# Second layer's dense pass with two buffers of turned rows, and shared score banks for the narrow diagonal heads of the first attention

## Chip, cores and metric

One core of a Trainium2 chip runs the whole program in one launch. The metric is the device time in microseconds (us). All products are float32: most are split into a high and a low part of a rounded 32-bit type (fp32r) and computed as three matmuls, high by high, low by high and high by low.

## What is computed

Two layers over 2048 rows of 512 numbers, each an attention and a feed-forward part with a layer norm after each. The change touches the first attention and the dense pass ahead of the second.

```python
# layer 0: 16 heads of 32, causal
scores = jnp.einsum('bhqd,bhkd->bhqk', q, k).astype(jnp.float32) * scale
causal = jnp.tril(jnp.ones((S, S), dtype=bool))
scores = jnp.where(causal, scores, jnp.finfo(jnp.float32).min)
attn = jax.nn.softmax(scores, axis=-1)
out = jnp.einsum('bhqk,bhkd->bhqd', attn, v)
...
# layer 1: one head of width 512, not causal, rotary in blocks of 128
q = (x @ q_w.T + q_b) * scale
kv = x @ kv_w.T + kv_b
k, v = (kv[..., :E], kv[..., E:])
q = _rope(q)
k = _rope(k)
```

## The kernel before

A tile is 128 rows, a chunk is 512 rows or four tiles; 2048 rows are 16 tiles or four chunks. Every engine has its own instruction stream, written out by hand, and semaphores order the streams. An engine takes its instructions strictly in the order written, so one that waits holds back all behind it.

**The first attention (layer0_attention).** There are 16 items, a query chunk c with a group g of four heads. A planner (attention0_plan) lists the steps of each item: step i scores one key tile kt against the item's 512 queries for the four heads, and the order interleaves four kinds of work. "scores" computes the transposed scores of one head (L838) into one of three banks, stb; "unit" computes a 128-row block of scores (L817) into another three banks, from which VectorE takes row maxima (L740, L745); "av" multiplies exponentials with values (L855), and "den" sums them (L876). Of the 160 steps 64 lie on the diagonal, 16 of each kind d = kt - 4c = 0, 1, 2, 3: they score 512, 384, 256 or 128 queries. On a diagonal step each head gets a second matmul (L843), which adds the mask of one 128x128 triangle by means of the identity matrix. ScalarE takes the exponential of each head from its bank (L702), and a head's first matmul waits until the exponential three heads back is done, which frees the bank. The av of step i-1 stands ahead of the fourth head of step i. GpSimd adds the exponentials of two steps (L668). The mask and the identity are fp32r.

**The dense pass (first part of layer1_attention).** First the layer norm of each tile: VectorE statistics (L906, L908), ScalarE root (L912), VectorE factors (L1846, L1848), ScalarE apply (L1696, in place in X). Then "turn": TensorE transposes the four 128x128 blocks of a tile (L1993) into a bank tb, ScalarE rounds them into the high part xch (L1705), VectorE subtracts for the low part xcl (L1854). xch and xcl hold one chunk. From a chunk TensorE computes eight "pieces" (12 matmuls each, 128 outputs by 512 rows, banks qk) and four "values" (12 matmuls each, 128 rows by 512, banks vb). Two pieces make a pair p. For each pair ScalarE copies both halves out with the bias (out, L1716), GpSimd multiplies by the cosines (L1657), VectorE by the sines (L1867), VectorE combines (L1874, L1875), ScalarE rounds (high, L1730), VectorE subtracts (low, L1884). Queries go to DRAM (L1616), keys stay in kth and ktl, and values go through the two buffers of vhl (L1738, L1888) to DRAM (L1605). The cosines and sines of a chunk, cs, have one buffer: SyncE loads those of the next chunk (L1624) behind the query stores of the chunk's fourth pair.

TensorE's order per chunk: eight pieces, turns n and n+1 of the next chunk, this chunk's values n-2 and n-1, turns n+2 and n+3, the next chunk's values n and n+1. A turn into xch waits for all pieces of the chunk before and for the value of the tile that it overwrites:

```python
if c > 0:
    act.wait_ge(s["qk_ok"], c * 2 * NP)
    act.wait_ge(s["v_ok"], k - TC + 1)
```

A piece waits until the copy and the sines of the piece four back are done, since it reuses that bank; a transposition waits for its tile's norm and for the low part of the tile two back; a value waits for the low part of the value two back.

Of the kernel before, what the change touches and what calls it, by code (L numbers as in the profile page):

```python
# [15 lines left out]
F32 = mybir.dt.float32  # L16
# [144 lines left out]
def layer0_qkv(nc, xT, w_qk, w_v, rope, masks, eye, X, V, hi, lo, qst, consts, qk_dram):  # L161
    with ExitStack() as ctx:
# [3 lines left out]
        maskf = m.sb("maskf", [P, P])  # L166
# [15 lines left out]
                 "t1_ok sin_ok sum_ok hi_ok lo_ok hstore0 hstore1 lstore0 lstore1 consts early0 early1").split()  # L182
# [34 lines left out]
        def _(sp):  # L217
# [16 lines left out]
            sp.dma_start(maskf[:], masks[:, 1, :]).then_inc(s["consts"], 16)  # L234
# [54 lines left out]
        def _(act):  # L289
# [17 lines left out]
            for what, c, j in acts:  # L307
# [33 lines left out]
                elif what == "v":  # L341
                    act.wait_ge(s["v_ok"], k + 1)
                    nc.scalar.activation(V[:, k, :], vb[:, k % 2, :], ACT.Copy).then_inc(s["vs_ok"], 1)
                    if k == TC:
                        act.wait_ge(s["consts"], 48)
                        nc.scalar.activation(identr[:], ident[:], ACT.Copy)
                        nc.scalar.activation(maskr[:], maskf[:], ACT.Copy)

        @block.vector
        def _(dve):  # L350
# [11 lines left out]
            nc.vector.memset(hidden[:, 0:CH - P], 0.0)  # L362
            split_half(0)
# [75 lines left out]


# [105 lines left out]
def layer0_attention(nc, stage_before, stored, landed, qx, qk_dram, m_dram, xs_dram, acc_dram, token, V, X, hi, lo, qst, consts, early, out_w, first_o):  # L546
# [14 lines left out]
    q_loads = [len([o for o in range(EARLY, n + 1) if q_slot[o] == q_slot[n]]) for n in range(NI)]  # L561

    with ExitStack() as ctx:
# [31 lines left out]
        def _(sp):  # L595
            def k_in(n, j, after):
                if after >= 0:
                    sp.wait_ge(s["st_ok"], 4 * (after + 1))
# [4 lines left out]
            def q_in(n, after):  # L603
                if after >= 0:
                    sp.wait_ge(s["st_ok"], 4 * (after + 1))
# [39 lines left out]
        def _(pool):  # L645
# [12 lines left out]
            for ev in order:  # L658
                if ev[0] == "av" and ev[1] % 2 == 0 and ev[1] + 1 < len(steps) - 1:
# [3 lines left out]
                    for a in range(2):  # L663
                        hs = slice(2 * a, 2 * a + 2)
                        pool.wait_ge(s["exp_ok"], 4 * (i + 1) + 2 * a + 2)
# [22 lines left out]
        def _(act):  # L688
            for ev in order:
                if ev[0] == "scores":  # L690
# [3 lines left out]
                    k = 4 * i + h  # L694
                    act.wait_ge(s["st_ok"], k + 1)
                    if i >= PSLOTS and h == 0:
# [5 lines left out]
                    nc.scalar.activation(probs[:, i % PSLOTS, h, w0:], stb[:, k % 3, w0:], ACT.Exp, scale=SCALE0)\  # L702
                        .then_inc(s["exp_ok"], 1)
# [7 lines left out]
                elif ev[0] == "prep":  # L711
                    k = ev[1]
                    if k == 0:
                        act.wait_ge(s["wo_in"], 16)
                        act.wait_ge(s["st_ok"], 4 * (final[NI - 2] + 1))
# [72 lines left out]
        def _(pe):  # L788
# [12 lines left out]
            for ev in order:  # L801
# [23 lines left out]
                elif ev[0] == "scores":  # L825
# [4 lines left out]
                    k = 4 * i + h  # L830
# [5 lines left out]
                    if k >= 3:  # L836
                        pe.wait_ge(s["exp_ok"], k - 2)
                    last = nc.tensor.matmul(  # L838
                        stb[:, k % 3, w0:],
                        kst[slot_of[n, kt // TC] % KSLOTS][0:97, h, kt % TC * P:(kt % TC + 1) * P],  # L840
                        qs[q_slot[n]][0:97, h, w0:], start=True, stop=kt < TC * c)
                    if kt >= TC * c:
                        last = nc.tensor.matmul(stb[:, k % 3, w0:w0 + P], identr[:], maskr[:], start=False, stop=True)  # L843
                    last.then_inc(s["st_ok"], 1)
                elif ev[0] == "av":
# [5 lines left out]
                    pe.wait_ge(s["exp_ok"], 4 * i + 4)  # L851
# [1728 lines left out]
```

## Time and profile before

| | |
|---|---|
| median of 3 runs | 2250.15 us (2246.75 to 2253.99) |
| the profiled execution: time | 2249.26 us |
| the profiled execution: span of the trace | 2247.5 us |
| TensorE busy | 2159.9 us, 96% |
| VectorE, ScalarE, GpSimd busy | 1180.8, 747.3, 669.3 us |
| first attention, 166 to 738 us | 572 us |
| dense pass after its first values, 1155.5 to 1311.6 us | 156.1 us |
| mean granted TensorE clock | 0.984 |

Matmuls overlap, and the end of each is modelled; so the text reads the distance from one start to the next start rather than a matmul's duration. A matmul that follows a wait is listed from about the moment the wait ended, with the load of its weights still ahead of it.

### The profile page before, as it was taken

The page shows a single profiled execution, that of the slowest core. Times are in us where ns is not written, and L with a number is a line of the kernel's source. Part 1 is how long each engine was busy: PE and PEld are TensorE (multiplying, and loading weights), DVE is VectorE, ACT ScalarE, POOL GpSimd, SP SyncE. Part 2 cuts the span into 40 slices and gives each one's busy share as a digit, 9 for nine tenths or more (in the row PEclk, how much of TensorE's full clock was granted, in tenths as well). Part 3 has the DMA queues.
Part 4 walks back from the last instruction along what each step waited for, and adds up shares of the span by engine and source line. Part 5 has one row for each costly group of instructions (what it writes and reads, how often), then busy time and mean ns, then how long its engine had stood idle before and what let it go on. Part 6 is the DMA issues. An engine that isn't in the chain of part 4 may idle for free. (4 is left out here: it accounts for less than half of the span.)

```text
span 2247.5 us, 27475 instructions
## 1 busy us (share of the span) xinstructions
PE 2159.9 (96%) x10148; PEld 1495.4 (67%) x10148; DVE 1180.8 (53%) x2305; ACT 747.3 (33%) x1344; POOL 669.3 (30%) x458
## 2 busy tenths in 40 slices
PE   7999999999999999999989999999999999999997
PEld 6866555555553654444477778888887888888886
DVE  5877777766662653222255642223235546554666
ACT  3425555555557322111144421111123211211223
POOL 4354555655557114432232340000003021212100
PEclk9989999999999999999999999999999999999999
DMA  5578345433310625655444350001101010100001
GB/s 181 185 195 198 96 124 126 103 85 72 67 29 21 251 107 220 138 95 92 75 133 150 131 215 23 25 19 29 38 1 57 1 38 20 38 19 26 12 19 57
DMA packets 104604, 197.27 MB, mean 88 GB/s; under 512 B 10384, under 2 KB 27664, under 8 KB 103056
## 3 DMA queue, kind: packets, MB, share of 16 engines
q1 hardware_dynamic: 92064, 162.78, 24.6%
q0 software_dynamic: 11408, 29.69, 5.8%
q10 hardware_dynamic: 1008, 3.15, 0.4%
q8 instruction: 78, 1.28, 0.2%
q14 instruction: 46, 0.38, 0.1%
HBM read 123.82 MB, written 71.75 MB: 87 GB/s over the span
## 5 line engine op out<-in xcount | busy, mean ns | idle before, releaser
L702 ACT ACTIVATE a_probs<-a_stb 128x512 f32<-128x512 f32 (+3 forms) x640 | 309.7, 535 | 238.5 <-PE a_stb L843 125.4
L668 POOL TENSOR_TENSOR a_probs<-a_probs 128x1024 f32<-128x1024 f32 (+3 forms) x158 | 277.9, 1772 | 245.7 <-PE a_avb L855 231.7
L740 DVE TENSOR_REDUCE a_mparts<-a_sbank 128x1 f32<-128x512 f32 x384 | 240.0, 683 | 86.3 <-PE a_sbank L817 85.9
L2220 POOL CAST m_wh<-wst 128x1024 fp32r<-128x1024 f32 x24 | 26.6, 1110 | 719.7 <-POOLq L1537 368.6
L57 PE MATMUL m_gu<-hi,m_wh 128*128 128x512 f32 x512 | 200.4, 391 | 3.0 <-DVE m_h L2350 1.6
L59 PE MATMUL m_gu<-hi,m_wl 128*128 128x512 f32 x512 | 199.8, 390 | 0.0
L58 PE MATMUL m_gu<-lo,m_wh 128*128 128x512 f32 x512 | 199.7, 390 | 0.0
L855 PE MATMUL a_avb<-a_probs,V 128*32 128x512 f32 (+3 forms) x1280 | 150.4, 542 | 0.7 <-ACT a_probs L702 0.7
L2299 DVE TENSOR_TENSOR m_h<-m_sg,m_gu 128x512 f32<-128x512 f32 x63 | 43.3, 687 | 193.8 <-ACT m_sg L2250 193.5
L745 DVE CUSTOM_DVE_ANT_0 a_junk<-a_sbank,hidden 128x128 bf16<-128x128 f32 (+3 forms) x256 | 113.2, 488 | 56.5 <-PE a_sbank L817 55.1
L2250 ACT ACTIVATE m_sg<-m_gu 128x512 f32<-128x512 f32 x64 | 38.3, 599 | 262.6 <-PE m_gu L59 262.6
L817 PE MATMUL a_sbank<-hi,q 96*128 96x512 f32 (+3 forms) x304 | 118.7, 415 | 5.8 <-DVE a_mparts L740 4.2
L838 PE MATMUL a_stb<-q,hi 97*128 97x512 f32 (+3 forms) x304 | 121.5, 408 | 1.4 <-ACT a_probs L702 1.1
L1822 ACT ACTIVATE pth<-q_tb 128x512 fp32r<-128x512 f32 x64 | 38.2, 598 | 246.2 <-PE q_tb L2079 246.2
L1959 DVE TENSOR_TENSOR ptl<-q_tb,pth 128x512 fp32r<-128x512 f32 x64 | 44.1, 691 | 143.4 <-ACT pth L1822 143.4
L817 PE MATMUL a_sbank<-lo,q 96*128 96x512 f32 (+3 forms) x288 | 109.1, 403 | 5.4 <-DVE a_mparts L740 3.3
L838 PE MATMUL a_stb<-q,lo 97*128 97x512 f32 (+3 forms) x288 | 110.3, 398 | 2.4 <-ACT a_probs L702 2.1
L57 PEld LDWEIGHTS m_gu<-hi,m_wh 128*128 128x128 f32 x512 | 96.5, 188 | 23.8 <-DVE m_h L2350 2.0
L58 PEld LDWEIGHTS m_gu<-lo,m_wh 128*128 128x128 f32 x512 | 96.6, 189 | 20.0
L59 PEld LDWEIGHTS m_gu<-hi,m_wl 128*128 128x128 f32 x512 | 96.4, 188 | 20.2
L1308 POOL DMA_INDIRECT acc<-e_rows_b,X x37 | 57.8, 1563 | 164.3 <-DVE e_rows_b L1432 131.2
L57 PE MATMUL q_vb<-vh,pth 128*128 128x512 f32 x256 | 102.6, 401 | 2.7 <-DMA vl<-v 2.7
(292 smaller groups left out, 4734.8 us busy)
## 6 DMA issues: line engine op xcount, KB each, us to landing
qk<-v_hl SPq DMA_DIRECT2D x32, 512.0 KB, 3.1
hi<-qk SPq DMA_DIRECT2D x60, 256.0 KB, 5.1
lo<-qk SPq DMA_DIRECT2D x60, 256.0 KB, 5.4
wst<-in_w_mlp SPq DMA_DIRECT2D x24, 512.0 KB, 3.5
q<-qk SPq DMA_DIRECT2D x42, 256.0 KB, 5.9
xs<-a_zeros POOLq DMA_DIRECT2D x39, 264.0 KB, 2.8
X<-xs SPq DMA_DIRECT2D x39, 264.0 KB, 2.7
v<-vhl SPq DMA_DIRECT2D x16, 512.0 KB, 5.3
```

Of the source, the lines that this page charges most:

```text
L57: nc.tensor.matmul(out, wh, xh, start=start, stop=False, skip_group_check=True)
L58: nc.tensor.matmul(out, wh, xl, start=False, stop=False, skip_group_check=True)
L59: return nc.tensor.matmul(out, wl, xh, start=False, stop=stop, skip_group_check=True)
L668: nc.gpsimd.tensor_tensor(probs[:, i % PSLOTS, hs, w0:], probs[:, i % PSLOTS, hs, w0:], probs[:, (i + 1) % PSLOTS, hs, w0:], ALU.add)\
L702: nc.scalar.activation(probs[:, i % PSLOTS, h, w0:], stb[:, k % 3, w0:], ACT.Exp, scale=SCALE0)\
L740: nc.vector.reduce_max(to, sbank[:, b, :], AX).then_inc(s["unit_max"], 1)
L745: nc.vector.tensor_tensor_reduce(out=junk[:, k % 2, 0:w], in0=sbank[:, b, 0:w], in1=hidden[:, CH - w:CH], scale=1.0, scalar=BIG, op0=ALU.a ...
L817: nc.tensor.matmul(bank[:, 0:w], qs[q_slot[n]][0:96, h, t * P:(t + 1) * P], kst[at % KSLOTS][0:96, h, 0:w], start=True, stop=True)\
L838: last = nc.tensor.matmul(stb[:, k % 3, w0:], kst[slot_of[n, kt // TC] % KSLOTS][0:97, h, kt % TC * P:(kt % TC + 1) * P], qs[q_slot[n]][0: ...
L855: last = nc.tensor.matmul(avb[HD0 * h:HD0 * (h + 1), w0:], V[:, kt, g * P + h * HD0:g * P + (h + 1) * HD0], probs[:, i % PSLOTS, h, w0:], ...
L1308: nc.gpsimd.indirect_dma_start(acc_dram[:, :], bass.IndirectOffsetOnAxis(ap=to[:, j:j + 1], axis=0), y[:, j % 2, :], None, compute_op=ALU. ...
L1959: nc.vector.tensor_tensor(ptl[:, 4 * g:4 * g + 4, :].rearrange("p a b -> p (a b)"), tb[:, (g + 1) % 2, :], f32(pth[:, 4 * g:4 * g + 4, :]) ...
```

## The change

In the dense pass a second pair of buffers holds turned rows: the part of kth and ktl that belongs to the last chunk's keys, which is written last. Even chunks use it, odd chunks use xch and xcl. A turn no longer waits for the pieces of the chunk before; from chunk 2 on it waits for the values of two chunks back. The order on TensorE per chunk becomes: pair 0, value, pair 1, turns n and n+1, value, pair 2, turns n+2 and n+3, pair 3, the other two values. Chunk 0 has only values 2 and 3 beside it, and chunk 3 only 12 and 13, with 14 and 15 after the first scores as before. ScalarE's, VectorE's and SyncE's orders follow.

In the first attention, steps with d=2 put two heads in one bank and steps with d=3 all four. The mask comes first, one matmul of 512 columns that reads the triangle and 128 columns of zeros repeatedly (d=2) or the triangle four times (d=3), and the heads' scores are added to it. One exponential of 512 columns then serves the bank. Semaphore counts go by banks ("groups") instead of heads. Identity and mask are bf16 now, the mask is 256 columns wide, and VectorE clears its second half once.

```diff
+        spare = [a[:, :, (NC - 1) * CH:] for a in (kth, ktl)]
+        def xc(c):
+            return spare if c % 2 == 0 else (xch, xcl)
+        def beside(c):
+            if c == 0:
+                return [2, 3]
+            return range(c * TC, c * TC + (TC if c + 1 < NC else 2))
...
+                if 1 <= p % NP < 3:
+                    v_out(beside(c)[p % NP - 1])
...
-                    for k in range(c * TC + 2, min(c * TC + TC + 2, NT)):
+                    for k in (*beside(c)[2:], *((NT - 2, NT - 1) if c + 1 == NC else ())):
                         v_out(k)
...
-                if c > 0:
-                    act.wait_ge(s["qk_ok"], c * 2 * NP)
-                    act.wait_ge(s["v_ok"], k - TC + 1)
+                if c >= 2:
+                    act.wait_ge(s["v_ok"], (c - 1) * TC)
... ScalarE, per chunk, as far as there is a next chunk
+                root(n); out(i); out(i + 1); apply(n); root(n + 1); high(p); apply(n + 1); value(v[0])
+                out(i + 2); out(i + 3); root(n + 2); apply(n + 2); turn(n); turn(n + 1); root(n + 3)
+                high(p + 1); apply(n + 3); value(v[1]); out(i + 4); out(i + 5); turn(n + 2); turn(n + 3)
+                high(p + 2); out(i + 6); out(i + 7); high(p + 3); value(v[2]); value(v[3])
... VectorE, per chunk
+                stats(n); sines(p); apply(n); stats(n + 1); sums(p); apply(n + 1); low(p); value(v[0])
+                sines(p + 1); stats(n + 2); sums(p + 1); apply(n + 2); stats(n + 3); turn(n); turn(n + 1)
+                apply(n + 3); low(p + 1); value(v[1]); sines(p + 2); sums(p + 2); turn(n + 2); turn(n + 3)
+                low(p + 2); sines(p + 3); sums(p + 3); low(p + 3); value(v[2]); value(v[3])
... TensorE, per chunk
+                for pair_no in range(NP):
+                    piece(2 * NP * c + 2 * pair_no)
+                    piece(2 * NP * c + 2 * pair_no + 1)
+                    if pair_no == 0:
+                        value(v[0])
+                    elif pair_no == 1:
+                        if more:
+                            turn(n)
+                            turn(n + 1)
+                        value(v[1])
+                    elif pair_no == 2 and more:
+                        turn(n + 2)
+                        turn(n + 3)
+                if more:
+                    for k in v[2:]:
+                        value(k)
... first attention
+def score_groups(items, steps):
+    group, done = {}, [0]
+    for i, (n, kt) in enumerate(steps):
+        per = {2: 2, 3: GH}.get(kt - TC * items[n][0], 1)
+        for h in range(GH):
+            group[i, h] = (done[-1] + h // per, h % per, per)
+        done.append(done[-1] + GH // per)
+    return group, done
...
-                    if k >= 3:
+                    if k >= 3 and j == 0:
                         pe.wait_ge(s["exp_ok"], k - 2)
...
+                    if per > 1 and j == 0:
+                        nc.tensor.matmul(stb[:, k % 3, :].rearrange("p (h n) -> p h n", h=per), identr[:],
+                                         maskr[:, 0:wide].unsqueeze(1).broadcast_to([P, per, wide]), start=True, stop=False,
+                                         skip_group_check=True)
+                    if per > 1:
+                        last = nc.tensor.matmul(stb[:, k % 3, j * wide:(j + 1) * wide], keys, asked, start=False, stop=j == per - 1,
+                                                skip_group_check=True)
...
-                                         (("hidden", CH, F32), ("identr", P, F32R), ("maskr", P, F32R)))
+                                         (("hidden", CH, F32), ("identr", P, BF16), ("maskr", 2 * P, BF16)))
```

The engines' orders are shown joined with semicolons here; in the code each call has its own line, and those on tiles n to n+3 are left out in chunk 3.

## Rows read from the trace of the kernel before

**Rows 1.** Windows: stretch, us, busy and instructions per engine, PEclk, DMA share, GB/s.

```profile
166.00:738.00 572.00, 551.87 (x3447) 292.44 (x3447) 371.99 (x901) 323.03 (x677) 319.51 (x216) 0.99 0.38 91
1155.50:1311.60 156.10, 147.81 (x649) 120.03 (x648) 97.80 (x155) 63.89 (x99) 57.60 (x40) 0.97 0.38 131
1187.80:1193.40 5.60, 5.60 (x13) 4.38 (x14) 3.02 (x4) 1.77 (x4) 0.00 (x0) 0.50 0.77 234
```

**Rows 2.** Timeline of TensorE from chunk 0 to 1: start, us, instruction, idle before.

```profile
1177.30 1.03 PE L1993 MATMUL q_tb<-ident,X 128*128 128x128 f32 x8
1178.09 0.47 PE L57 MATMUL q_vb<-q_wh,q_xch 128*128 128x512 f32 x1
...
1183.43 0.39 PE L59 MATMUL q_vb<-q_wh,q_xcl 128*128 128x512 f32 x1
1185.36 1.23 PE L1993 MATMUL q_tb<-ident,X 128*128 128x128 f32 x8 [1.54 <-DVE q_xcl L1854]
1187.76 0.76 PE L57 MATMUL q_vb<-q_wh,q_xch 128*128 128x512 f32 x1 [1.17 <-DVE vhl L1888]
...
1193.45 0.47 PE L58 MATMUL q_vb<-q_wl,q_xch 128*128 128x512 f32 x1
```

**Rows 3.** Timeline of TensorE from chunk 1 to 2.

```profile
1225.90 1.23 PE L1993 MATMUL q_tb<-ident,X 128*128 128x128 f32 x8 [1.56 <-DVE q_xcl L1854]
1228.30 0.76 PE L57 MATMUL q_vb<-q_wh,q_xch 128*128 128x512 f32 x1 [1.18 <-DVE vhl L1888]
...
1230.99 0.47 PE L57 MATMUL q_vb<-q_wh,q_xch 128*128 128x512 f32 x1
```

**Rows 4.** Groups by line, dense pass: busy us, mean ns, idle before.

```profile
L1657 POOL TENSOR_TENSOR q_turned<-q_qkf,q_cs 128x512 f32<-128x512 f32 x32 | 46.9, 1470 | 114.2 <-ACT q_qkf L1716 114.2
L1696 ACT ACTIVATE X<-X,minus,norm_rstd 128x512 f32<-128x512 f32 x12 | 9.5, 812 | 5.6 <-DVE minus L1848 5.6
```

**Rows 5.** Timeline of all engines, from chunk 0 to 1.

```profile
1188.14 1.63 SPq L1616 DMA_DIRECT2D q<-qhl  x2
...
1189.86 0.46 SPq L1624 DMA_DIRECT2D q_cs<-in_rope  x1
...
1199.81 0.75 DVE L1867 SCALAR_TENSOR_TENSOR q_across<-q_qk,bqk,q_cs 128x512 f32<-128x512 f32 x1 [0.97 <-ACT q_qkf L1716]
...
1206.36 1.04 ACT L1730 ACTIVATE qhl<-q_turned 128x1024 fp32r<-128x1024 f32 x1
```

**Rows 6.** DMA issues ahead of chunks 1 and 3: KB each, median us to landing.

```profile
q_cs<-in_rope SPq DMA_DIRECT2D x1, 512.0 KB, 5.0
...
q_cs<-in_rope SPq DMA_DIRECT2D x1, 512.0 KB, 7.2
```

**Rows 7.** Timeline of TensorE, wide heads, with and without a mask.

```profile
390.70 0.39 PE L838 MATMUL a_stb<-q,lo 97*128 97x512 f32 x1
...
390.99 0.45 PE L817 MATMUL a_sbank<-hi,q 96*128 96x512 f32 x1
391.28 0.39 PE L838 MATMUL a_stb<-q,lo 97*128 97x512 f32 x1
...
416.74 0.40 PE L838 MATMUL a_stb<-q,hi 97*128 97x512 f32 x1
...
417.21 0.40 PE L838 MATMUL a_stb<-q,hi 97*128 97x512 f32 x1
```

**Rows 8.** Timeline of TensorE, narrow heads of a step with d=3.

```profile
412.99 0.27 PE L838 MATMUL a_stb<-q,lo 97*128 97x128 f32 x1
413.10 0.28 PE L843 MATMUL a_stb<-maskr,identr 128*128 128x128 f32 x1
413.43 0.33 PE L838 MATMUL a_stb<-q,lo 97*128 97x128 f32 x1
```

**Rows 9.** Groups by line and shape, exponentials of the first attention.

```profile
L702 ACT ACTIVATE a_probs<-a_stb 128x512 f32<-128x512 f32 x448 | 243.1, 600 | 138.6 <-PE a_stb L838 107.7 <-PE a_stb L843 28.1
...
L702 ACT ACTIVATE a_probs<-a_stb 128x128 f32<-128x128 f32 x64 | 16.7, 278 | 33.7 <-PE a_stb L843 32.8
```

More of the change, by code:

```diff
@@ L693, in _ @@
                     w0 = max(0, kt - TC * items[n][0]) * P
[L694 removed]
+                    k, j, per = group[i, h]
+                    if j < per - 1:
+                        continue
                     act.wait_ge(s["st_ok"], k + 1)
[L696 removed]
+                    if i >= PSLOTS and h == per - 1:
                         act.wait_ge(s["av_ok"], i - PSLOTS + 1)
@@ L1928, in _ @@
             for c in range(NC):
-                n, p = (c + 1) * TC, c * NP
-                for t, tiles in enumerate(((n,), (n + 1, n + 2), (n + 3,))):
-                    sines(p + t)
-                    for k in tiles if c + 1 < NC else ():
-                        stats(k)
-                    sums(p + t)
-                    for k in tiles if c + 1 < NC else ():
-                        apply(k)
-                    low(p + t)
-                sines(p + 3)
-                if c + 1 < NC:
+                n, p, more = (c + 1) * TC, c * NP, c + 1 < NC
+                v = beside(c)
+                if more:
+                    stats(n)
+                sines(p)
+                if more:
+                    apply(n)
+                    stats(n + 1)
+                sums(p)
+                if more:
+                    apply(n + 1)
+                low(p)
+                value(v[0])
+                sines(p + 1)
+                if more:
+                    stats(n + 2)
+                sums(p + 1)
+                if more:
+                    apply(n + 2)
+                    stats(n + 3)
                     turn(n)
                     turn(n + 1)
-                sums(p + 3)
-                if c + 1 < NC:
-                    value(n - 2)
-                    low(p + 3)
-                    value(n - 1)
+                    apply(n + 3)
+                low(p + 1)
+                value(v[1])
+                sines(p + 2)
+                sums(p + 2)
+                if more:
                     turn(n + 2)
                     turn(n + 3)
-                    value(n)
-                    value(n + 1)
+                low(p + 2)
+                sines(p + 3)
+                sums(p + 3)
+                low(p + 3)
+                if more:
+                    for k in v[2:]:
+                        value(k)
                 else:
-                    low(p + 3)
                     peak(0)
```

135 lines of the change are left out of this document (67 added, 68 removed).

## The prediction

> **What bounds the kernel now.** I read the page first: TensorE is busy for 96% of the span, the others for 53% at most. A busy TensorE is not one at its peak, so next I read windows of the two stretches that the change touches, and in them the distances between starts. In the dense pass TensorE is busy for 147.8 of 156.1 us, while VectorE has 97.8 us of work and ScalarE 63.9 [rows 1]. So TensorE sets the end, and what others cost is only what it waits for them. The timeline shows where: at each of the three passages from a chunk to the next, ahead of turns n+2 and n+3 and ahead of the value behind them. In the first attention TensorE has 551.9 us in 572, VectorE 372, GpSimd 320, ScalarE 323 [rows 1]; there too I count its matmuls first and its waits second.
>
> **Dense pass: what is removed.** The value matmul at 1183.43 is the 24th since 1178.09, so their distance is 5.34/23 = 0.23 us, and the next instruction could start at 1183.66. The turns start at 1185.36: 1.70 us late. Eight transpositions take 0.79 us when nothing is waited for (1177.30 to 1178.09), here the value behind them starts 2.40 us after them: 1.61 us more [rows 2]. Together 3.3 us. Behind it the granted clock is 0.50, which is 1.2 GHz of 2.4 [rows 1]: from 1187.76 to 1193.45 lie 13 matmuls in 5.69 us, at full clock 13 x 0.23 = 3.0, so 2.7 us more [rows 2]. From chunk 1 to 2 the two waits are the same (1.56 and 1.18 us listed as idle, against 1.54 and 1.17), and six matmuls take 2.69 us instead of 1.4: 1.3 us more [rows 2, 3]. The third passage shows the same waits and no fall of the clock. The sum is 3 x 3.3 + 2.7 + 1.3 = 13.9 us. No matmul is added or removed here: 32 pieces, 14 values and 48 transpositions stay.
>
> The waits arise because the turns of the next chunk begin only when the last piece is through, and ScalarE and VectorE then have the last pair, two turns and a value to handle in one queue. With the second buffer the turns stand within the chunk, 2.7 to 8 us of matmuls apart from what reads them, and a value's low part is due two values later. If the other engines keep up, all 13.9 us go.
>
> **Dense pass: what is late next.** I follow the chain from the last piece of chunk 0, called time 0. Two things that before lay in the passage's slack now matter. First, cs has one buffer and SyncE asks for the next chunk's only behind the query stores of the fourth pair. That pair still has to pass ScalarE's copy, GpSimd (1.47 us a half), two VectorE sums (about 1.3 together), high (1.04) and low (1.2): about 5.3 us, more with a pair of other work in the queues. Behind it come two store issues (1.63 together) and the cs issue [rows 4, 5]. I put the issue at 7 us (before it was at 1189.86 - 1177.30 = 12.6) and its landing 5.0 us later [rows 2, 6], 0.3 more for the issue: 12.3. Before, the first reader came at 1199.81, 10 us behind the issue, so nobody waited [rows 5]. After, chunk 1's first piece is through at 2.7 us, since chunk 0 has no values left at its end. VectorE's and GpSimd's queues stand at the first sines and cosines until 12.3.
>
> Second, what is queued behind them: on VectorE apply(8), stats(9), sums(4), apply(9); on ScalarE apply(8), root(9), high(4), apply(9). From 12.3: two cosines 2.8 us, sums 1.3, VectorE's factors 0.4, with ScalarE's high (1.04) beside them, apply 0.81 and some 0.4 of semaphores: the norm of tile 9 is ready at about 18.3. TensorE has until then pieces 8 and 9, value 4, pieces 10 and 11: 60 matmuls x 0.227 = 13.6 us (0.227 is 5.34/23 less the start behind the transpositions). Turn 9 waits for 18.3, so 4.2 us are lost, in two parts (turn 8 about 1.2, turn 9 about 3.0). Turns 10 and 11 follow 0.5 us late. At the next passage two values (5.4 us) stand at the end of the chunk, the cs issue is at about 8.4 and the chain ready at 19.7 against 19.0 us of matmuls: 0.7 us, and 0.5 again behind it. Chunk 3 has no turns. So 5.9 us come back as waits. The gap in chunk 1 is as long as the 3.3 us behind which the clock fell in two of three cases, by 2.7 and 1.3 us; I take the mean over three cases, 1.3. The dense pass gains 13.9 - 5.9 - 1.3 = 6.7 us. Bounds: 12.4 if cs is no obstacle (TensorE then has 28.8 us per chunk 0 against some 24 of VectorE's work, and I keep 1.5 for single late turns); and 0 if cs lands after 7.2 us, as it did ahead of chunk 3 [rows 6], which adds 1.9 us at each passage, and the clock falls twice (5.9 + 3.8 + 4.0 = 13.7).
>
> The stores of the middle values move ahead on SyncE, between the row loads and the fourth pair's stores. Each waits for the low part of its value, which is through 2 us or more before the fourth pair's high; behind them wait only rows for two chunks later. GpSimd's queue keeps its order. Chunk 3's end, with the first scores, values 14 and 15 and the loads behind them, keeps its order too, so the waits at the start of the second attention should stay as they are.
>
> **First attention: the masks.** What does a mask cost? From one wide head to the next there are 0.58 us with a mask and a unit between, and 0.47 with a unit alone: 0.11 us [rows 7]. That is more than 128 columns need (a quarter of 0.23 is 0.06). In the narrow step starts follow each other by 0.11 as well [rows 8]: a matmul of 128 columns is too short to cover the load of the next weights, and this load sets the distance. Before, 64 diagonal steps have four masks each. After:
> - d=0 and d=1 (32 steps): the same masks in bf16. The load that is not covered is that of the next fp32r weights, so nothing changes.
> - d=2 (16 steps): four masks of 0.11 become two of 512 columns, 0.23 each: 0.44 against 0.46, nothing.
> - d=3 (16 steps): four of 0.11 become one of 0.23: 0.21 less, 16 times, 3.4 us.
>
> **First attention: the exponentials.** ScalarE does 2 x 0.600 instead of four exponentials at d=2, and one of 0.600 instead of 4 x 0.278 at d=3 [rows 9]. It isn't the bound, so the work itself is worth nothing; its times are. The third narrow head starts 0.33 us after the mask before it instead of 0.11 [rows 8]: it waits for the wide exponential three heads back. With four heads in one bank this wait falls away: 0.22 x 16 = 3.5 us. In exchange the last exponential of a narrow step ends later, by 0.32 us at d=3 and about 0.22 at d=2, and the third head of the next step waits for its bank. It stands two heads and mostly two units (0.9 us) behind, while the chain from the last score to the free bank is about 1 us: I take 0.1 us for each of 32 steps, 3.2 us; bounds are 0 and the whole lateness, 16 x 0.32 + 16 x 0.22 = 8.6. GpSimd's sum of a step with d=3 waits for the whole bank, but is then only 128 columns wide and needed two steps later. Sum: -3.4 - 3.5 + 3.2 = -3.7 us, bounds -6.9 and +1.7. The memset and the wider cast at the start lie under the first weights' loads.
>
> **The sum.** 2249.26 us of the profiled execution, less 6.7, less 3.7: 2238.9. That execution is 0.9 us under the median of the runs shown, and I leave that out: 2239.
>
> **The rivals.**
> - The cs load is no obstacle, or the clock stays up: dense pass -12.4, attention -3.7, 2233 us. For it: SyncE may be earlier than my 7 us. Against it: from the fourth pair's last piece five operations and two stores stand in line, whatever else happens. 0.20.
> - The new waits take the whole dense gain: 2245.6. For it: the cs landing of 7.2 us, and that the clock fell behind 3.3 us of waits. 0.14.
> - The identity's weights load faster in bf16 and this load was the uncovered one: each of the 128 masks at d=0 and d=1 costs 0.06 instead of 0.11, 6.4 us more gain, 2232.5. Against it: the uncovered load stands behind the mask. 0.06. The Trainium skill says in "TensorE: Matmul & The Clock Gate", section "Weight-path perf modes", that weights of 128 columns in a type other than FP32 are read by a faster path. By that rule masks would be cheaper; by rows 7 and 8 the rule can be right and change nothing.
> - Slower: the change of type between fp32r scores and the bf16 mask keeps TensorE from loading weights ahead. The nearest price is the uncovered load, 0.11 us. There are 128 + 32 + 16 = 176 masks; it decides from 10.4/176 = 0.06 us for each, and gives 2258 at 0.11 for one change and 2278 for both. The trace before shows no bf16 matmul; fp32r to the plain transpositions costs nothing visible at 1177.30 [rows 2]. 0.07.
> - The late exponentials cost their whole 8.6 us: 2244. 0.05.
>
> **How the numbers follow.** The forecast's own case is 2235 to 2243 with a chance of 0.48: cs landing 1 us sooner or later, and the clock. A measurement here can tell 0.3%, which is 6.8 us: below 2243.4 counts as faster. The forecast and the first and third rival lie there (0.48 + 0.20 + 0.06, less 0.02 at the edge), and of the second a fifth: 0.75. Within 0.3%: the rest of the second, the exponentials, the edge: 0.18. Slower: 0.07. For 8 in 10 the range goes from 2231 to 2247.
>
> **What would show it.** In the profile after, the idle time ahead of turns n+2 and of the value behind them should be gone at all three passages. In chunk 1 turns 8 and 9 should wait for L1696, some 4 us together, with VectorE's first L1867 of each chunk listed behind the DMA of cs and the cs issue some 7 to 8 us behind the last piece of the chunk; the clock may fall there. From the first piece of chunk 0 to value 15 I expect 149 us instead of 156.1. In the attention 572 us should become 568, the wide mask should stand 0.23 us ahead of the first narrow score, and a mask between two wide matmuls should still cost 0.11. The prediction is wrong if cs is read without a wait, if masks cost more than 0.11, or if the start of the second attention waits longer for its values.

## The result and the profile after

The changed kernel takes 2236.84 us (median of 6 runs, 2234.01 to 2240.82) against 2249.67 us for the kernel before on the same chip (6 runs, 2246.75 to 2253.99). The ratio is 0.994, 95% interval 0.9926 to 0.9954: 10 to 17 us less. The forecast was 2239. The profiled execution took 2238.97 us, with a span of 2237.2 and a mean granted clock of 0.983, against 2249.26 and 0.984 before.

The page after, part 1 and the clock's row of part 2:

```profile
PE 2156.0 (96%) x10068; PEld 1467.6 (66%) x10068; DVE 1183.7 (53%) x2306; ACT 736.8 (33%) x1264; POOL 664.7 (30%) x458
...
PEclk9988999999999999999999999999999999999999
```

TensorE's busy time moved by 4 us only, and its share is still 96%: the page alone doesn't tell where 10 us went. Windows do, cut at the same instructions as before. The first row is the attention, the second the dense pass from the first piece of chunk 0 to value 15, the third a stretch behind turn 9 (TensorE's value 5). Columns as in [rows 1].

```profile
167.00:734.00 567.00, 548.04 (x3363) 263.24 (x3366) 373.20 (x897) 311.60 (x597) 318.30 (x214) 0.99 0.39 92
1156.60:1305.50 148.90, 144.51 (x648) 119.53 (x648) 96.87 (x155) 65.90 (x101) 55.60 (x41) 0.98 0.41 142
1205.25:1210.50 5.25, 5.25 (x14) 4.12 (x13) 4.71 (x10) 1.70 (x4) 2.52 (x2) 0.50 0.96 286
```

Measured from matmul to matmul, the attention (first score to last denominator) went from 569.9 to 566.0 us and the dense stretch from 155.8 to 148.9. Together 10.8, where the profiled difference is 10.3; the stretches between and behind hold unchanged code, and what they scatter by (below) nearly cancels here.

The waits of TensorE in the dense stretch; of before these were L1993 behind L1854 and L57 behind L1888, at each of the three passages [rows 2, 3]:

```profile
PE q_tb L2047 <- ACT X L1737: 4.4, 2, 2.5
```

All six old waits are gone, and one new pair is there, 4.4 us in two waits. The timeline of all engines shows the chain that leads to it (L1665 is the cs issue, L1698 the cosines, L1907 the sines, L1888 the norm's factors, L1737 apply, L2047 the turns):

```profile
1190.60 1.62 SPq L1655 DMA_DIRECT2D q<-qhl  x2
...
1192.32 0.45 SPq L1665 DMA_DIRECT2D q_cs<-in_rope  x1
...
1198.69 1.41 DVE L1907 SCALAR_TENSOR_TENSOR q_across<-q_qk,bqk,q_cs 128x512 f32<-128x512 f32 x2 [5.97 <-DMA q_cs<-in_rope]
...
1198.73 2.50 POOL L1698 TENSOR_TENSOR q_turned<-q_qkf,q_cs 128x512 f32<-128x512 f32 x2 [10.65 <-DMA q_cs<-in_rope]
...
1200.45 0.81 ACT L1737 ACTIVATE X<-X,minus,norm_rstd 128x512 f32<-128x512 f32 x1 [6.25 <-DVE minus L1888]
...
1201.32 0.66 PE L2047 MATMUL q_tb<-ident,X 128*128 128x128 f32 x4 [1.88 <-ACT X L1737]
...
1203.63 0.80 ACT L1737 ACTIVATE X<-X,minus,norm_rstd 128x512 f32<-128x512 f32 x1
...
1204.48 1.12 PE L2047 MATMUL q_tb<-ident,X 128*128 128x128 f32 x4 [2.50 <-ACT X L1737]
```

Read it downwards: two query stores hold SyncE, the cs issue comes 1.7 us behind the first of them, VectorE and GpSimd both stop for the transfer, and the norm of tile 9, which stands behind the sines in VectorE's queue, reaches TensorE last. From 1203.7 us, still within the wait for turn 9, to 1210.5 the granted clock is 0.50, which is 1.2 GHz of 2.4; the third window is the part of it in which TensorE works on value 5.

### The profile page after: what moved, and what is told of

Same layout as the page of the kernel before. It is cut to its first block and busy times, and to the rows that moved or that the text cites. A ratio compares the mean times of both kernels' runs of the same rounds, so it can differ in the third digit from the quotient of the medians.

```text
span 2237.2 us, 27233 instructions
## 1 busy us (share of the span) xinstructions
PE 2156.0 (96%) x10068; PEld 1467.6 (66%) x10068; DVE 1183.7 (53%) x2306; ACT 736.8 (33%) x1264; POOL 664.7 (30%) x458
## 5 line engine op out<-in xcount | busy, mean ns | idle before, releaser
L722 ACT ACTIVATE a_probs<-a_stb 128x512 f32<-128x512 f32 (+1 forms) x560 | 298.3, 588 | 248.5 <-PE a_stb L868 104.9
L759 DVE TENSOR_REDUCE a_mparts<-a_sbank 128x1 f32<-128x512 f32 x384 | 240.4, 682 | 83.2 <-PE a_sbank L836 82.5
L57 PE MATMUL m_gu<-hi,m_wh 128*128 128x512 f32 x512 | 199.8, 390 | 3.5 <-DVE lo L2350 1.9
L57 PEld LDWEIGHTS m_gu<-hi,m_wh 128*128 128x128 f32 x512 | 96.1, 188 | 24.0 <-DVE lo L2350 2.1
L868 PE MATMUL a_stb<-q,hi 97*128 97x512 f32 (+1 forms) x256 | 107.9, 429 | 2.1 <-ACT a_probs L722 1.1
L57 PE MATMUL q_vb<-vh,pth 128*128 128x512 f32 x256 | 102.1, 399 | 2.8 <-DMA vl<-v 2.8
L57 PE MATMUL m_yb<-m_wh,m_hh 128*128 128x512 f32 x256 | 102.1, 399 | 2.8 <-DVE X L2364 2.7
```

The lines of the kernel that those rows point to most:

```text
L57: nc.tensor.matmul(out, wh, xh, start=start, stop=False, skip_group_check=True)
L722: nc.scalar.activation(to, got, ACT.Exp, scale=SCALE0).then_inc(s["exp_ok"], 1)
L759: nc.vector.reduce_max(to, sbank[:, b, :], AX).then_inc(s["unit_max"], 1)
L868: last = nc.tensor.matmul(stb[:, k % 3, w0:], keys, asked, start=True, stop=kt < TC * c)
```

## The experiments

Two measures are used. The dense stretch is as above. For the attention a second one turned out to be needed: between its first score and VectorE's first full-width reduction (L740, L759 after) lies a stretch in which the clock is below full for part of the time. The fall begins at 152 to 155 us, ahead of the first score, and its length differs from one execution to the next: it is 23.9 us in e11 and 34.1 in e10 below, whose instructions are equal in number and size. Here are two windows each of the kernel before, and of the run below that has bf16 masks and no shared banks:

```profile
166.30:189.70 23.40, 22.41 (x123) 16.30 (x123) 15.13 (x69) 11.61 (x26) 7.97 (x9) 0.78 0.84 201
189.70:737.70 548.00, 529.45 (x3325) 276.14 (x3325) 356.34 (x832) 311.42 (x652) 311.26 (x206) 1.00 0.36 86
```

```profile
167.00:192.60 25.60, 25.48 (x122) 15.07 (x120) 14.97 (x66) 11.49 (x25) 7.18 (x8) 0.63 0.81 184
192.60:740.60 548.00, 529.38 (x3325) 254.93 (x3325) 356.62 (x832) 311.51 (x652) 311.38 (x206) 1.00 0.36 86
```

The second windows both end 0.6 us behind the last denominator and are equally long; the first differ, and with them the clock (0.78 against 0.63). From first score to that reduction the runs took 22.3 to 26.4 us. So the attention is also given from that reduction to the last denominator, called the steady attention. It leaves out the first item's four steps, so it holds 15 of the 16 steps of each kind on the diagonal. One other fall of the clock lies in it in four of the runs, about 130 us in: from the 80th to the 100th reduction they take 30.5 to 30.8 us where the same code without a fall takes 29.0 to 29.3, and these 1.5 us are taken off where it says so.

| kernel | dense stretch | attention | steady attention | time |
|---|---|---|---|---|
| before | 155.8 | 569.9 | 547.4 | 2249.67 |
| after | 148.9 | 566.0 | 542.6 | 2236.84 |
| e1 dense part alone | 146.0 | 572.3 | 547.2 (1.5 off) | 2239.49 |
| e2 attention part alone | 156.1 | 566.5 | 542.7 | 2243.23 |
| e3 after, cs issued early | 141.4 | 566.3 | 542.4 | 2230.29 |
| e4 after, cs in two places | 141.4 | 566.2 | 542.6 | 2232.66 |
| e5 after, no shared banks | 146.0 | 573.8 | 547.4 | 2241.23 (one run) |
| e6 after, sharing at d=3 only | 146.3 | 567.5 | 543.3 (1.5 off) | 2232.81 (one run) |
| e7 after, sharing at d=2 only | 146.3 | 569.9 | 547.1 | 2239.11 (one run) |
| e8 as e6, masks in fp32r | 144.8 | 565.3 | 542.0 | 2229.74 (one run) |
| e9 e3 and e8 together | 141.4 | 565.9 | 542.1 (1.5 off) | 2230.34 |
| e10 as e9, d=2 too, masks last | 141.4 | 568.3 | 541.1 (1.5 off) | 2232.09 |
| e11 as e10, one start a bank | 141.4 | 564.7 | 541.2 | 2231.59 |

Steady attentions of the same code agree within 0.3 us (before, e1; after, e2, e3, e4), where whole ones differ by 2.4. Stretches of unchanged code scatter too: from the last denominator to the first turn 406 to 412 us, from value 15 to the feed-forward part 379 to 384. So single spans can't separate 2 us, stretches can. The dense stretch of the changed order is given as it was, with its clock; of that order as it stands in the changed kernel there are six profiles (after, e1 and e5 to e8), from 144.8 to 148.9 us, 146.4 in the mean.

**e1 and e2: each part alone.** The kernel before, with one function of the changed one.

```diff
 e1: layer1_attention as changed, layer0_attention as before
-                if c > 0:
-                    act.wait_ge(s["qk_ok"], c * 2 * NP)
-                    act.wait_ge(s["v_ok"], k - TC + 1)
+                if c >= 2:
+                    act.wait_ge(s["v_ok"], (c - 1) * TC)
...
 e2: layer0_attention as changed, layer1_attention as before
+                    if per > 1 and j == 0:
+                        nc.tensor.matmul(stb[:, k % 3, :].rearrange("p (h n) -> p h n", h=per), identr[:],
...
```

> The kernel before with the changed dense pass alone, first attention as before. If the two parts are independent and the forecast's terms hold, the stretch from the first piece to the last value takes 149 us (156.1 before, 149.1 changed), the first attention keeps its 570 us, and the ratio is about 0.997. If the gain of the whole change came mostly from the attention, the ratio is within 0.1% of 1.

> The kernel before with the changed first attention alone. By the forecast's terms the attention shortens by about 4 us (as it did from 569.9 to 566.0), the dense pass keeps its 156 us, ratio 0.998. A rival says that the 4 us of one trace are scatter: then the stretch is as long as before.

The dense part alone gives a ratio of 0.9957 (0.994 to 0.9974), 5.8 to 13.5 us less; the attention part alone 0.997 (0.9953 to 0.9988), 2.7 to 10.6 us less. By the stretches the dense part is worth 9.8 us here and the attention part 4.7 (steady): neither needs the other. In e1 the waits on the norm are 2.9 us and TensorE's busy time is 1.8 over the 141.4 of e3 below, in the changed kernel 4.4 and 3.1. That is why the 149 us expected of e1 became 146.0. The cs load explains the waits: from issue to landing it took 6.3 us in the changed kernel and 4.8 in e1, and turn 8 waited for 1.88 and 0.32 us; turn 9 waited for 2.50 and 2.55.

**e3: cs issued ahead of the query stores.** Nothing else moves; the wait on the readers of the old cs stays.

```diff
+                if p % NP == NP - 1 and c + 1 < NC:
+                    sp.wait_ge(s["cos_ok"], 2 * p + 2)
+                    sp.wait_ge(s["sin_ok"], 2 * p + 2)
+                    sp.dma_start(cs[:], rope[:, :, (c + 1) * CH:(c + 2) * CH].rearrange("a p n -> p a n"))\
+                        .then_inc(s["csload"], 16)
                 if which == 0:
...
-                    if c + 1 < NC:
-                        sp.wait_ge(s["cos_ok"], 2 * p + 2)
-                        sp.wait_ge(s["sin_ok"], 2 * p + 2)
-                        sp.dma_start(cs[:], rope[:, :, (c + 1) * CH:(c + 2) * CH].rearrange("a p n -> p a n"))\
-                            .then_inc(s["csload"], 16)
```

> The changed kernel, with the load of the next chunk's cosines and sines issued ahead of the query stores of the chunk's fourth pair, right behind the last reader, instead of behind them. Theory of the late cs: the issue comes some 4 us earlier, the waits of turns 8 and 9 (4.4 us listed) shrink to under 1 us, the clock stays up there, and the dense stretch takes about 142 to 143 us instead of 149.1. Rival, VectorE's queue is too full beside chunk 0 and sets turns 8 and 9 anyway: the waits stay above 2.5 us. A second rival is that the store of queries, now behind the load, is late for the next rounding of queries: then ScalarE's high of the next chunk's first pair waits for a DMA.

2230.29 us (4 runs, 2229.3 to 2232.59), ratio 0.991 (0.988 to 0.9939), 6.6 us under the changed kernel's median. The two were not run in one series, and the intervals of their ratios overlap (0.9926 to 0.9954 for the changed kernel), so the stretch has to decide. The dense stretch fell by 7.5 us from the profile after, by 5.0 from the mean of the six. Its window, and the cs issue and its readers in the timeline:

```profile
1156.95:1298.35 141.40, 141.40 (x649) 117.39 (x648) 96.83 (x155) 65.74 (x101) 55.69 (x42) 1.00 0.43 150
```

```profile
1188.41 0.38 SPq L1655 DMA_DIRECT2D q_cs<-in_rope  x1
...
1194.06 1.41 DVE L1907 SCALAR_TENSOR_TENSOR q_across<-q_qk,bqk,q_cs 128x512 f32<-128x512 f32 x2 [1.04 <-ACT q_qkf L1756]
1194.09 2.55 POOL L1698 TENSOR_TENSOR q_turned<-q_qkf,q_cs 128x512 f32<-128x512 f32 x2 [5.71 <-ACT q_qkf L1756]
```

TensorE is busy for all of the 141.40 us at a granted clock of 1.00, and the readers of cs wait for ScalarE's copy, no more for the DMA. Counted from the last piece of chunk 0, the issue comes 4.2 us earlier than in the changed kernel, and the load lands in 3.8 us. The second rival, a late query store, is out too: ScalarE waits for no DMA in this stretch. 4.4 us of waits and the 3.1 behind them, which is what is left of 148.9 - 141.4, both hung on that one transfer. There is little to spare: the norm of tile 9 is through at 1199.84, and turn 9, the second half of the eight transpositions from 1199.57 on, starts at 1200.01.

**e4: cs in two places.** Chunk 1's cosines and sines have their own space, loaded at the start of the pass, so that the load of chunk 2's can be issued a chunk early; chunk 3's has the old order.

```diff
-        cs = m.sb("cs", [P, 2, CH])
+        cs_main = m.sb("cs", [P, 2, CH])
+        cs_one = spare_cs[:, :, 2 * CH:3 * CH]
+        cs_of = (cs_main, cs_one, cs_main, cs_main)
...
-                    if c + 1 < NC:
+                    if c in (0, 2):
```

> The changed kernel with a second place for cosines and sines: chunk 1's are loaded at the start, into rows of the low key part that are written only in chunk 2; chunk 2's are loaded at the end of chunk 0; chunk 3's as before. Theory of the late cs: no reader of chunks 1 and 2 waits for the DMA, turns 8 and 9 wait 1.5 us at most, dense stretch 141 to 143 us, as with the early issue or up to 1 us shorter. If VectorE's queue is the cause, turns 8 and 9 still wait over 2.5 us.

2232.66 us (5 runs), ratio 0.992 (0.9895 to 0.9946), dense stretch 141.4: the same as e3. A rival to "the stores hold the issue back" was that the early issue only disturbs less; a quite different way of having cs in time gives the same stretch to 0.1 us. The rival that VectorE's queue sets turns 8 and 9 is out by both runs: neither turn waits. VectorE still waits 4.3 us for cs ahead of chunk 3, where no turns follow, and TensorE doesn't notice.

**e5 to e7: bf16 masks without sharing, sharing at one d.** One number in score_groups decides.

```diff
-        per = {2: 2, 3: GH}.get(kt - TC * items[n][0], 1)
 e5
+        per = 1
 e6
+        per = {3: GH}.get(kt - TC * items[n][0], 1)
 e7
+        per = {2: 2}.get(kt - TC * items[n][0], 1)
```

> The changed kernel with one head to a bank throughout, so of the attention's change only the bf16 identity and mask are left. The first attention from its first score to its last sum took 569.9 and 572.3 us in the two traces of the old form, 566.0 to 566.5 in four of the new. Forecast: the type changes nothing, 570 to 572. The rival of faster bf16 weights: 128 + 128 masks at 0.06 instead of 0.11 us, 557 to 559. A mask between two wide matmuls costs 0.11 us in the first case, 0.06 in the second.

> The changed kernel with banks shared only where four narrow heads fit (d=3); d=2 as before. Forecast's terms: -3.4 for three masks' worth, -3.5 for the wait of the third head, +1.6 for the late exponential: 566 us or a little less, so nearly the whole gain. If the gain came from the fewer exponentials at d=2 as well, over 568.

> The changed kernel with banks shared only at d=2 (two heads); d=3 as before. Forecast's terms: masks 0.44 against 0.46 us per step, nothing, and +1.6 for the late exponential: 571 to 573 us. If fewer exponentials help by themselves, 568 to 569.

By the whole stretch e5 looks 3.9 us slower than before, and that would be a price of bf16. The windows above say otherwise: the difference lies in the first 26 us, where the clock was lower, and the steady attention is 547.4 in both. Of e5 there is one execution, so that the masks have no part in its lower clock is likely and not shown. Masks in bf16 between fp32r scores cost nothing and save nothing in the steady part. Sharing at d=3 gives 4.1 us there. At d=2 it gives 0.3 alone, which is no more than the scatter, and 0.7 beside d=3. So e7 shows no loss of 1.6 us, against its expectation, and the whole stretches of e5 and e6 lie above theirs by the clock.

Where a d=3 step gains, TensorE's timeline shows. Before, the first three heads of such a step up to the av; after, the same step:

```profile
412.58 0.40 PE L817 MATMUL a_sbank<-lo,q 96*128 96x512 f32 x1
412.82 0.22 PE L838 MATMUL a_stb<-q,lo 97*128 97x128 f32 x1
412.88 0.28 PE L843 MATMUL a_stb<-maskr,identr 128*128 128x128 f32 x1
...
413.70 0.44 PE L817 MATMUL a_sbank<-lo,q 96*128 96x512 f32 x1
414.08 0.64 PE L855 MATMUL a_avb<-a_probs,V 128*32 128x512 f32 x4
```

```profile
412.33 0.40 PE L836 MATMUL a_sbank<-lo,q 96*128 96x512 f32 x1
412.58 0.39 PE L861 MATMUL a_stb<-maskr,identr 128*128 128x512 bf16 x1
412.62 0.64 PE L865 MATMUL a_stb<-q,lo 97*128 97x128 f32 x3
413.09 0.45 PE L836 MATMUL a_sbank<-lo,q 96*128 96x512 f32 x1
413.47 0.64 PE L884 MATMUL a_avb<-a_probs,V 128*32 128x512 f32 x4
```

From the unit ahead of the step to the av: 1.50 us before (with the gap ahead of the third head, 413.10 to 413.43 in [rows 8]), 1.14 after. Over whole steps, from one av to the next, the gain isn't the same everywhere. Of the twelve such stretches in chunks 1 to 3 that hold the first three heads of a step with d=3, six are shorter in e6 than in e5 by 0.32 or 0.33 us, three by 0.17 to 0.29 and three by about 0.1. The stretch behind, with the fourth head, is mostly shorter by another 0.08.

At d=2 the masks alone account for what moved in e7. Here are the starts in e5, from the first head of such a step to its next av, and from its fourth head to the next wide head; below them those in e7:

```profile
539.15 0.28 PE L868 MATMUL a_stb<-q,hi 97*128 97x256 f32 x1
...
540.17 1.06 PE L884 MATMUL a_avb<-a_probs,V 128*32 128x512 f32 x8
...
542.02 0.38 PE L868 MATMUL a_stb<-q,hi 97*128 97x256 f32 x1
542.25 0.23 PE L870 MATMUL a_stb<-maskr,identr 128*128 128x128 bf16 x1
...
542.61 0.40 PE L868 MATMUL a_stb<-q,hi 97*128 97x512 f32 x1
```

```profile
536.44 0.39 PE L861 MATMUL a_stb<-maskr,identr 128*128 128x512 bf16 x1
...
537.58 1.06 PE L884 MATMUL a_avb<-a_probs,V 128*32 128x512 f32 x8
...
539.43 0.38 PE L865 MATMUL a_stb<-q,hi 97*128 97x256 f32 x1
...
539.88 0.40 PE L868 MATMUL a_stb<-q,hi 97*128 97x512 f32 x1
```

Up to the av it is 1.02 us in e5 and 1.14 in e7, which has two wide masks there; behind it 0.59 and 0.45, since the fourth head of e7 has no mask. The same pair, 0.08 to 0.13 longer and 0.12 to 0.14 shorter, stands at most steps with d=2, and the next step's heads start no later.

**e8: the masks of e6 in fp32r.** Sharing at d=3 only, since a mask of 256 columns in fp32r doesn't fit beside the rest.

```diff
-                                         (("hidden", CH, F32), ("identr", P, BF16), ("maskr", 2 * P, BF16)))
+                                         (("hidden", CH, F32), ("identr", P, F32R), ("maskr", P, F32R)))
```

> As the run with banks shared only at d=3, but identity and mask in fp32r as they were before (the mask 128 columns wide). If the type is worth nothing either way, the attention takes the same within 0.5 us, and a mask matmul of 512 columns stands 0.23 us ahead of its first score in both. If bf16 weights help where the mask opens a bank, this one is longer by up to 16 x 0.05 = 0.8 us and more at the 128 other masks (6 us).

The steady attention is 542.0, 1.3 us less than e6 in bf16, where less than 0.5 was expected; e9 below has the same attention and 542.1. It comes in pieces of 0.03 to 0.07 us over many steps, with no one place. In the step shown above the two types take the same time from unit to av (1.13 and 1.14). So bf16 costs nothing in e5 and some 1.3 us beside shared banks; why only there stays open. The dense stretch of this run is the shortest of the six, because the granted clock is 1.00 in all of it, with waits of 2.9 us as in e1.

**e9: e3 and e8 together.** Both diffs above.

> The cs load ahead of the query stores in the dense pass, and in the attention one bank only for d=3, with masks in fp32r. If the two gains are independent, as the single runs of each part suggest, the dense stretch is 141.4 us and the attention 565.3, together 1.0 us less than with the early load alone (2230.3): 2229 us. The rival: the bf16 masks with d=2 sharing lose nothing by the median, the 1.0 us is scatter, and the time is that of the early load alone, 2230 to 2233.

2230.34 us (6 runs, 2222.61 to 2238.88), ratio 0.9905 (0.9885 to 0.9925). The stretches are 141.4 and 542.1, as each alone. By the time alone it can't be told from e3: both are 2230.3.

**e10: d=2 as well, the mask behind the heads.** This kernel changes part of the computation: with a start of its own for each head, the masks of a shared bank are not added to its earlier heads. Its instructions and their sizes are those of a kernel with the whole computation.

```diff
-                    if per > 1 and j == 0:
-                        nc.tensor.matmul(stb[:, k % 3, :].rearrange("p (h n) -> p h n", h=per), identr[:],
-                                         maskr[:, 0:wide].unsqueeze(1).broadcast_to([P, per, wide]), start=True, stop=False,
...
-                        last = nc.tensor.matmul(stb[:, k % 3, j * wide:(j + 1) * wide], keys, asked, start=False, stop=j == per - 1,
+                        last = nc.tensor.matmul(stb[:, k % 3, j * wide:(j + 1) * wide], keys, asked, start=True, stop=False,
+                        if j == per - 1:
+                            last = nc.tensor.matmul(stb[:, k % 3, :].rearrange("p (h n) -> p h n", h=per)[:, :, 0:P], identr[:],
+                                                    maskr[:, 0:P].unsqueeze(1).broadcast_to([P, per, P]), start=False, stop=True,
```

> As the run before it, with d=2 in shared banks as well, and the mask of a shared bank added behind its heads, in 128 columns of each head only (fp32r, 256 columns at d=2 and 512 at d=3), instead of ahead of them in the bank's full width. No zeros are added. If matmul columns and loads alone count, d=2 has two masks of 256 columns (about 0.12 us each) instead of four of 0.11: 0.2 us less in each of 16 steps, 3.2 us, and sharing at d=2 gave 1.5 us more beside d=3 in bf16: the attention goes from 565.3 to about 561, the time to about 2225. The rival: what sharing a bank gained came from the exponentials, and a mask at the end of a bank keeps them back by its own 0.12 to 0.23 us and another 0.1 of load, so that the third head of the next step waits longer: then attention stays at 565 or goes up to 567, and the time is 2229 to 2232.

By the whole attention, 568.3, the rival seemed right. It isn't: 3.5 us of that lie in the first stretch, where this execution took 25.8 us and e9 22.3 at a higher clock. The steady attention is 541.1, 1.0 less than e9, not the 4 us expected and not a loss. Summed from av to av, the two kinds of steps go opposite ways. At d=2 (two masks of 256 columns instead of four of 128) the 15 steps are 3.0 us shorter together, which is the 3.2 expected of them. At d=3, where e9 has its mask first, the stretches with the first three heads are 1.5 us shorter, but those with the fourth head, behind which the mask now stands, 3.6 longer: 2.1 us lost. e11 against e8 gives the same sums to 0.1 us. So mask last is the better order at d=2 and the worse one at d=3. Last at d=2 and first at d=3 was not run; by these sums it is worth some 2 us more, an estimate. 2232.09 us (5 runs), ratio 0.9915 (0.9901 to 0.9929).

**e11: the same with one start for each bank.**

```diff
-                        last = nc.tensor.matmul(stb[:, k % 3, j * wide:(j + 1) * wide], keys, asked, start=True, stop=False,
+                        last = nc.tensor.matmul(stb[:, k % 3, j * wide:(j + 1) * wide], keys, asked, start=j == 0, stop=False,
```

> As the run before it (early cs load, banks shared at d=2 and d=3, fp32r masks of 128 columns for each head, added last), but only the first head of a bank starts an accumulation; the others are written with start=False into columns that nothing has written since. The Trainium skill says in "PSUM" that a start clears the written marks of the whole bank and that a later matmul without one overwrites where the mark is clear and adds where it is set; by that the scores and masks come out as in the reference, without a bank-wide mask of zeros ahead. The instructions are the same in number and size as in the run before. If columns and loads alone count, TensorE's time from VectorE's first reduction of the attention to its end is that of the run before, 541.0 us once 1.5 us of a fall of the clock are taken off (542.1 with d=3 alone, 542.6 in the changed kernel), the dense stretch is 141.4, and the time 2229 us. The rival: the time depends on the start flag, and the stretch is longer by more than 1 us.

The steady attention is 541.2 and the dense stretch 141.4, so the flag costs no time. 2231.59 us (6 runs, 2229.26 to 2233.8), ratio 0.992 (0.9906 to 0.9933). By the stretches this is the best of the kernels run with the whole computation (1.4 us less attention than the changed kernel, 7.5 less dense pass than its profile); by the times e3, e9 and e11 are one, with medians 5 to 7 us under the changed kernel's, from separate series.

## Why the prediction was right, point by point

**The waits removed.** Forecast 13.9 us from 3 x 3.3 and two falls of the clock. In e3, which has the changed order and no new wait, 155.8 became 141.4: 14.4 us, all of the old waits and of their clock. Right.

**The new wait, its place and its chain.** Count from 1185.66, where the last piece of chunk 0 is through (24 matmuls of 0.227 ahead of the value at 1191.11). Forecast: cs issue at +7, first reader at +12.3, tile 9's norm at +18.3. Measured: 1192.32 is +6.7, 1198.69 is +13.0, and the apply that ends at 1204.43 is +18.8. Turns 8 and 9 waited for 1.88 and 2.50 us as listed, 4.4 against 4.2. The mechanism is right, and e3 and e4 show the cause. The size owes something to luck: the transfer took 6.3 us where 5.0 was taken. In the five other profiles of this code it took 4.7 to 5.0, as the forecast has it; there the norm of tile 9 is ready at +17.1 to +17.4, about 1 us before the forecast's time, and the two turns wait for 2.7 to 3.1 us.

**The later waits.** Forecast 1.7 us (0.5 behind turn 9, 0.7 and 0.5 at the next passage). None is there: two values at the end of chunk 1 cover the chain. Counted from the last piece of chunk 1, the turn that needs tile 13's norm stands at +19.5 us, and the norm is ready at +17.5 in the changed kernel and +19.0 in e8. That term was too large, and with it the 5.9, which is 4.4 in the changed kernel and 2.7 to 3.1 in five profiles with the same dense code (e1 and e5 to e8).

**The clock.** Forecast 1.3 as a mean of three cases. TensorE's busy time is 3.1 us over 141.4 in the changed kernel, 1.8 or 1.9 in e1, e5, e6 and e7, and 0.5 in e8. In e8 the granted clock is 1.00 in the whole stretch, so 0.5 us of each is taken for something else than the clock, at the waits. That leaves 2.6 for the clock in the changed kernel, 1.3 or 1.4 in four and nothing in e8, in the mean 1.3, as forecast.

**The dense pass in sum.** -6.7 was forecast and -6.9 measured, but only in the profile after, which had the slowest cs load and the longest fall of the clock of the six. Over all six the gain is 6.9 to 11.0 us, 9.4 in the mean, and the mis-sized term is the waits (5.9 against 3.2 in the mean of the six). The lower bound has a slip of its own: a landing of 7.2 us instead of 5.0 adds 2.2 at each passage, not 1.9, which makes the losses 14.3 instead of 13.7 and leaves the bound at no gain.

**Masks in bf16.** Forecast 0 for those between wide heads: right, 547.4 in e5 and before. The Trainium skill's rule on weights of another type than FP32 ("TensorE: Matmul & The Clock Gate", section "Weight-path perf modes") showed no effect on the time here. The trace agrees with it on the loads: a mask's load is listed with 98 ns in e5 and 190 before (medians), TensorE's load time fell from 276.1 to 254.9 us in the windows of the two, and the busy time of its matmuls stayed at 529.4. The rival that a change of type costs 0.06 us or more each is out: 0.00 in e5, and 0.01 at the most over all masks (1.3 us over the 208 of e6).

**Sharing at d=3.** Forecast 0.21 for masks, 0.22 for the third head's wait, less 0.1 for later exponentials: 0.33 for each step. Measured 4.1 us in all in bf16 and 5.4 in fp32r, which is 0.27 and 0.36 for each of the 15 steps in it, unevenly spread as shown above. Right in sum.

**Sharing at d=2.** Forecast a loss of 0.1 in each of 16 steps, 1.6 us. Measured a gain of 0.3 to 0.7. This is the step of the attention's sum that was mis-sized: the late exponential was to hold back the third head of the next step by 0.1 us, and in e7 the next step starts its heads no later than in e5 (the stretch with them is 0.12 to 0.14 shorter, about a mask). The sum, -3.7, stands against -3.9 in the whole stretch and -4.8 in the steady part, the rest being the first stretch, 22.5 us before and 23.4 after, with its clock.

**The whole time.** The forecast, 2239, met the profiled execution's 2238.97; the median is 2236.84, 2 us less. With 9.4 and 4.8 us, the mean dense gain and the steady attention's, the sum gives 2235. So the mechanisms were right and put the time in the range, and that it met the profile to the microsecond is luck. The start of the second attention kept its wait for values, 2.8 us against 2.7.

## What to carry to other kernels

When an order is tightened, look at what the removed slack had covered: here a transfer with one buffer, issued behind two stores, cost nothing before and 3.4 to 7.5 of 14.4 us after, and a few lines of SyncE's order gave it back. Add the price of the clock behind each new wait of some microseconds on TensorE, as a range and not only as a mean: here it was 0 to 2.6 us in six profiles of one code. Before a forecast is called exact, look whether other profiles of the same code give the same number. Compare short stretches cut at the same instructions and at full clock: here a whole attention stretch moved by 3.9 us while its steady part stayed the same.

## What the runs showed of the hardware

- Sharing one bank between several heads needs one start alone. The Trainium skill says in "PSUM — Partial Sum Buffer", section "The four PSUM rules", that a start clears the written marks of its whole bank, and that a matmul without one overwrites where the mark is clear. No trace shows the marks themselves; e11, whose computation is whole only by that rule, rests on it and saves the bank-wide mask of zeros, with no change of the time from the flag (steady attention 541.1 and 541.2).
- In the changed kernel TensorE waited for 1.88 and 2.50 us with 0.7 us of work between, and the granted clock was 0.50 for 6.8 us, from 0.8 us before the second wait ended. In four other profiles, with waits of up to 0.5 and of 2.5 us, it was 0.50 for 3.4 us, and in e8, with the same waits, it stayed at 1.00. The price was 2.6, 1.3 to 1.4 and 0 us.
- The load of 512 KB for cs (chunk 0 to 1) took 4.7 to 6.3 us behind two query stores in six profiles, and 3.7 to 3.9 us ahead of them in four (e3, e9, e10, e11). The two store issues held SyncE for 1.6 us.
- A mask's weights of 128 columns were loaded in 98 ns in bf16 and in 190 ns in fp32r, and the steady attention took the same time with either (547.4, e5 and before).
- At the start of the attention the granted clock was 0.50 for 23.9 us in one execution and for 34.1 in another with equal instructions (e11 and e10), and the stretch up to the first full reduction took 23.5 and 25.8 us.
